# Where the first batch's stacked keys and queries come from: part-by-part copies within SBUF, or scratch memory

## What is computed

```
q = (h @ wq.T + bq_).reshape(bh, sl, H, DH)
k = (h @ wk.T + bk_).reshape(bh, sl, H, DH)
scores = jnp.einsum('blhd,bmhd->bhlm', q, k) * inv_sqrt_d
w_avg = jax.nn.softmax(scores, axis=-1).mean(axis=1)
new_w = jax.nn.softmax(CSCALE * w_avg + rel[None], axis=-1)
sa = jnp.einsum('blm,bme->ble', new_w, h)
```

## Time and profile before

| what | us |
|---|---|
| median of three executions | 2780.65 |
| lowest, highest | 2773.95, 2781.83 |
| span of the profiled execution, first to last instruction | 2799.2 |
| last scatter of expert rows issued by POOL | 504.86 |
| fence matmul | 506.05 |
| first score matmul | 514.52 |
| last score matmul starts | 2661.6 |

### The profile page before, as it was taken

The page is one execution under the profiler, slowest core; times in us unless marked ns, Lnnn a source line. Parts: engine busy times, 40 slices in busy tenths (PEclk is TensorE's granted clock), DMA queues, the critical chain, the costliest instruction groups (busy, mean ns, idle before and its releaser), DMA issues.

```text
span 2799.2 us, 93828 instructions
## 1 busy us (share of the span) xinstructions
PE 2390.9 (85%) x38289; PEld 1272.3 (45%) x38289; DVE 2454.6 (88%) x3428; ACT 2303.4 (82%) x4212; POOL 1447.9 (52%) x2877
## 2 busy tenths in 40 slices
PE   5778777689898999999899998999989988989856
PEld 3445365234444444444444454444444444444435
DVE  4887944699998999999999999999999998999956
ACT  5887634489898999999999999999999988989832
POOL 3445553235654566445664466644665446643564
PEclk8898887699999999999999999999999999999977
DMA  4000023322212121221212212122131221210000
GB/s 134 1 1 1 23 78 94 75 44 50 47 20 47 37 58 33 34 47 35 59 30 37 48 33 61 24 43 46 32 63 20 48 42 36 41 26 11 2 1 16
DMA packets 49198, 110.44 MB, mean 39 GB/s; under 512 B 7424, under 2 KB 42112, under 8 KB 44480
## 3 DMA queue, kind: packets, MB, share of 16 engines
q1 hardware_dynamic: 40384, 96.31, 17.2%
q0 software_dynamic: 2432, 5.08, 0.6%
q10 hardware_dynamic: 5952, 3.04, 0.4%
HBM read 79.41 MB, written 29.05 MB: 39 GB/s over the span
## 4 chain that ended last, share of the span: by engine, by line
PE 41%; issue 18%; ACT 12%; DVE 11%; POOL 8%; DMA 1%; ACTq 0%; SPq 0%; DVEq 0%; POOLq 0%
PE bank L773 13%; PE bank L704 12%; PE bank L784 11%; ACT E L1046 9%; DVE NM L1423 7%; ACT acc L997 1%; POOL acc L1644 1%; POOL H L1654 1%; PE bank L685 1%; POOL H L1657 1%; PE bank L698 1%; POOL smp L1637 1%; ACT UB L1008 1%; POOL dg L1702 1%; PE bank L747 0%
## 5 line engine op out<-in xcount | busy, mean ns | idle before, releaser
L1423 DVE TENSOR_REDUCE NM<-bank 128x1 f32<-128x1024 f32 x1536 | 1800.3, 1207 | 97.0 <-PE bank L773 76.5
L1046 ACT ACTIVATE E<-bank,NM 128x1024 f32<-128x1024 f32 x1536 | 1709.0, 1119 | 198.1 <-DVE NM L1423 153.1
L773 PE MATMUL bank<-KS,QS 72*32 72x512 bf16 x12288 | 977.7, 390 | 173.7 <-ACT E L1046 118.5
L784 PE MATMUL bank<-E,dg 128*32 128x256 f32 x12288 | 943.7, 387 | 8.0 <-issue 6.2
L1702 POOL TENSOR_TENSOR dg<-mask,RZ 128x128 f32<-128x128 f32 x384 | 153.7, 400 | 871.9 <-DVE RZ L1433 766.8
L773 PEld LDWEIGHTS bank<-KS,QS 72*32 72x32 bf16 x12288 | 263.2, 96 | 713.4 <-ACT E L1046 583.9
L784 PEld LDWEIGHTS bank<-E,dg 128*32 128x32 f32 x12288 | 394.6, 112 | 300.4 <-issue 75.3
L1046 ACT ACTIVATION_READ_ACCUMULATOR E<-bank,NM 128x1 f32 x1536 | 310.0, 202 | 0.0
L1644 POOL TENSOR_TENSOR acc<-acc,rel 128x256 f32<-128x256 f32 x384 | 272.8, 731 | 7.8 <-ACT acc L997 7.8
L704 PE MATMUL bank<-H,ET 128*32 128x129 f32 x6144 | 193.8, 276 | 9.7 <-DVE ET L1366 6.3
L704 PE MATMUL bank<-hT,WL 128*32 128x256 f32 x2304 | 166.5, 389 | 29.0 <-ACT UB L1008 21.9
(11 more groups left out here) (265 smaller groups left out, 2639.1 us busy)
## 6 DMA issues: line engine op xcount, KB each, us to landing
KS<-scratch SPq DMA_DIRECT2D x72, 384.0 KB
QS<-scratch SPq DMA_DIRECT2D x216, 128.0 KB
scratch<-UB SPq DMA_DIRECT2D x144, 128.0 KB
WL<-in_wl SPq DMA_DIRECT2D x6, 1091.0 KB, 12.4
first<-in_fill SPq DMA_DIRECT2D x2, 990.0 KB, 8.1
second<-in_fill SPq DMA_DIRECT2D x2, 990.0 KB, 10.3
UNITB<-second ACTq DMA_DIRECT2D x2, 528.0 KB
W<-in_moe_w SPq DMA_DIRECT2D x1, 1032.0 KB
```

Source lines behind the costliest of these rows:

```text
L773: inst = PE_.matmul(bank[x % 3][32 * i:32 * i + 32, k * 512:k * 512 + 512], QS[0:72, half % 2, 4 * hq + i, r0:r0 + 32], KS[0:72, b, k, 4 * ...
L784: inst = PE_.matmul(pb(6)[32 * k:32 * k + 32, 256 * grp:256 * grp + 256], dg[:, x // 4 % 3, x % 4, :], E[:, x % NE, :].rearrange("p (i k c ...
L1046: A_.activation(E[:, x % NE, :], bank[x % 3][:, :], ACT.Exp, bias=NM[:, x % 4:x % 4 + 1], accum_out=ZS[:, quad % 3, j:j + 1]).then_inc(s[" ...
L1423: V.tensor_reduce(NM[:, x % 4:x % 4 + 1], bank[x % 3][:, :], AX.X, ALU.max, negate=True).then_inc(s["rowmax"], 1)
```

## The change

For halves 0 and 1, SP no longer stores the parts and reads them back. New functions `place_k` and `place_q` issue nine DMAs each, from a plane of `PQ` (128 partitions of 1 KB) straight to 8 partitions of `KS` or `QS` (16 KB each). So that a plane's partitions lie in the order in which the stack takes them (all heads of dimension 0, then of dimension 1, ...), the columns of the weights and the biases are permuted on the host (`by_d`). The stores of later halves then write DRAM in the order in which it lies, without a swap. All waits are counted anew; `part0` of half 1, and the first of POOL's pieces for half 2, wait for the copies' own semaphores.

```diff
+        def stacked_k(b, l):
+            return 48 * (l + 1) + (96 if b == 0 else 0)
+        def stored(n):
+            return 96 * (n - 1)
...
                 if k:
                     e.wait_ge(s["parts"], 4 * n + 18)
                 elif n > -4:
-                    e.wait_ge(s["pq_store"], 96 * (4 + n))
+                    e.wait_ge(s["stackk00"], 144)
+                    e.wait_ge(s["stackq00"], 144)
...
                     e.wait_ge(s["pjo"], 2 * n + 10)
-                    e.wait_ge(s["pq_store"], 96 * (4 + n))
+                    if n == -2:
+                        e.wait_ge(s["stackk01"], 144)
+                        e.wait_ge(s["stackq01"], 144)
+                    else:
+                        e.wait_ge(s["pq_store"], stored(3 + n))
...
+            e.wait_ge(s["split"], before_half(n - 4) + 16)
             for j in range(3):
-                if n < 2:
-                    e.wait_ge(s["parts"], 4 * n + (1, 3, 4)[j])
-                else:
-                    e.wait_ge(s["split"], before_half(n - 4) + 16)
                 for k in range(2):
-                    e.dma_start(scr[b, hf, k, j].rearrange("d h t -> h d t"), PQ[:, 2 * j + k, :]).then_inc(s["pq_store"], 16)
+                    e.dma_start(scr[b, hf, k, j], PQ[:, 2 * j + k, :]).then_inc(s["pq_store"], 16)
+
+        def place_k(e, n):
+            for j in range(3):
+                e.wait_ge(s["parts"], 4 * n + (1, 3, 4)[j])
+                for i in range(3):
+                    r0 = 24 * i + 8 * j
+                    e.dma_start(KS[r0:r0 + 8, 0, n, :, :], PQ[:, 2 * j + 1, :]).then_inc(s[f"stackk0{n}"], 16)
+
+        def place_q(e, n):
+            for i in range(3):
+                e.wait_ge(s["parts"], 4 * n + (1, 3, 4)[i])
+                for j in range(3):
+                    r0 = 24 * i + 8 * j
+                    e.dma_start(QS[r0:r0 + 8, n, :, :], PQ[:, 2 * i, :]).then_inc(s[f"stackq0{n}"], 16)
...
             for n in range(2, HALF_N):
-                stack_q(e, n - 1)
+                if n > 2:
+                    stack_q(e, n - 1)
                 store_qk(e, n)
...
             mixed_of(0)
-            store_qk(e, 0)
-            stack_k(e, 0)
-            stack_q(e, 0)
-            store_qk(e, 1)
-            stack_k(e, 1)
+            place_k(e, 0)
+            place_q(e, 0)
+            place_k(e, 1)
+            place_q(e, 1)
             mixed_of(1)
             fence_sp(e, 1)
```

More of the change, by code:

```diff
@@ L764, in scores @@
                 if x % 128 == 0:
-                    e.wait_ge(s[f"stackk{b}0"], 48 * (l + 1))
-                    e.wait_ge(s[f"stackk{b}1"], 48 * (l + 1))
+                    e.wait_ge(s[f"stackk{b}0"], stacked_k(b, l))
+                    e.wait_ge(s[f"stackk{b}1"], stacked_k(b, l))
                 if x % 64 == 0:
@@ L1004, in post_act @@
                 if fc == 0:
-                    e.wait_ge(s["pq_store"], 96 * min(4 + n, HALF_N))
+                    e.wait_ge(s["pq_store"], stored(min(3 + n, HALF_N - 1)))
                     if n:
@@ L1755, in stack_k @@
             l, b, hf, u = unit(n)
-            e.wait_ge(s["pq_store"], 96 * (n + 1))
+            e.wait_ge(s["pq_store"], stored(n))
             if l:
@@ L1764, in stack_q @@
             l, b, hf, u = unit(n)
-            e.wait_ge(s["pq_store"], 96 * (n + 1))
-            if n >= 2:
-                e.wait_ge(s["scores"], 64 * (n - 1))
+            e.wait_ge(s["pq_store"], stored(n))
+            e.wait_ge(s["scores"], 64 * (n - 1))
             for i in range(3):
@@ L1776, in store_qk @@
                 e.wait_ge(s[f"stackq{b}{hf}"], 144 * l)
-                e.wait_ge(s[f"stackk{b}{hf}"], 48 * l)
+                e.wait_ge(s[f"stackk{b}{hf}"], stacked_k(b, l - 1))
+            e.wait_ge(s["split"], before_half(n - 4) + 16)
             for j in range(3):
-                if n < 2:
-                    e.wait_ge(s["parts"], 4 * n + (1, 3, 4)[j])
-                else:
-                    e.wait_ge(s["split"], before_half(n - 4) + 16)
                 for k in range(2):
-                    e.dma_start(scr[b, hf, k, j].rearrange("d h t -> h d t"), PQ[:, 2 * j + k, :]).then_inc(s["pq_store"], 16)
+                    e.dma_start(scr[b, hf, k, j], PQ[:, 2 * j + k, :]).then_inc(s["pq_store"], 16)
[11 more added lines that the diff above has]
+                    e.dma_start(QS[r0:r0 + 8, n, :, :], PQ[:, 2 * i, :]).then_inc(s[f"stackq0{n}"], 16)
         def rows_of(e, r):
@@ L1916 @@
     q = "L1_attn_"
+    by_d = np.arange(128).reshape(16, 8).T.reshape(128)
     wl = np.concatenate([
-        g[q + "Wq"].transpose(0, 2, 1), g[q + "Wk"].transpose(0, 2, 1), g[q + "W1"].transpose(0, 2, 1),
+        g[q + "Wq"].transpose(0, 2, 1)[:, :, by_d], g[q + "Wk"].transpose(0, 2, 1)[:, :, by_d], g[q + "W1"].transpose(0, 2, 1),
         g[q + "W2"].transpose(0, 2, 1).reshape(6, 4, 128, 128).transpose(0, 2, 1, 3).reshape(6, 128, 512),
@@ L1921 @@
           ("ln1_w", "ln1_b", "ln2_w", "ln2_b", "ln3_w", "ln3_b", "b2")],
-        g[q + "bq"][:, :, None], g[q + "bk"][:, :, None], g[q + "b1"].reshape(6, 4, 128).transpose(0, 2, 1),
+        g[q + "bq"][:, by_d, None], g[q + "bk"][:, by_d, None], g[q + "b1"].reshape(6, 4, 128).transpose(0, 2, 1),
     ], axis=2)
```

## The result

In nine runs each on one chip the changed kernel took **2791.30 us** (2781.94 to 2807.70), the kernel before 2781.83 us (2773.95 to 2790.61). The medians lie 9.5 us apart. The forecast was +13.4.

A forecast was written before the change was run, and what follows sets the result against it. The prediction took the bound to be the 8.28 us idle before the first score, waiting for half 1's keys. 17.9 + 2 - 8.1 + 1.6 = +13.4 us on the median 2780.65 gave 2794 us, range 2773 to 2807.

The forecast's parts named there:

- forecast case: Copies at the seam take 1.29 to 2.08 us each: +4.4 to +27 us, 2785 to 2808; chance 0.5.
- Term 1: At the seam, ACT's first piece of half 1 waits for half 0's 18 copies: 502.35 instead of 484.45, +17.9 us.
- d: Time of one 128 KB copy into 8 partitions when copies run back to back, taken as 1.7 us.
- the middle of a range between a quiet and a crowded row: Copy time taken between query reads in a crowded queue (1.29 us) and with nothing else about (2.08): 1.7 us.
- Term 2: After ACT's wait, PE restarts at the low clock, slowing two to three expert units: +2 us.
- Term 3: The idle before the first score matmul goes, since half 1's keys land ahead of the fence: -8.1 us.
- one of the signs that I had named as wrong: At the first score, a wait for `KS` still ahead of it would show the forecast wrong.
- Term 4: The load of Y stands behind half 1's 18 copies in SP's queue, so DVE waits for it: +1.6 us.
- The later halves at no cost: Unswapped stores in the 22 later halves change no time, since existing waits cover them: 0 us.
- Rival A: Copies at the seam are fast (up to 1.02 us each), ACT waits 0 to 5.7 us: 2772.5 to about 2779; chance 0.25.
- Rival B: Copies run at the query reads' quiet rate throughout, 2.08 us each, Y late by 8.4: +27 us, 2808; chance 0.2.

The follow-up runs named there:

- e2: The changed kernel with half 1's parts in a buffer of their own, so ACT waits for no copy: 2794.50 us, 0.9993 of the kernel before.
- e13: The changed kernel with each copy going into 8 partitions spaced 9 apart instead of 8 neighbours: 2766.67 us, 0.9946 of the kernel before.
- e6: The changed kernel with 36 more copies of 128 KB, in four destination shapes, while the DMA engines are idle: 2794.09 us in one run.
- e1: The changed kernel with Y loaded before half 1's nine query copies, not after: 2802.14 us, 1.0019 of the kernel before.
- e9: The kernel before with each half's nine query reads into 8 partitions written as three into 24: 2772.78 us, 0.9975 of the kernel before.
- e10: The kernel before with three wide query reads per half and unswapped stores with permuted weights: 2763.71 us, 0.9943 of the kernel before.

## Why the prediction was right, and where it was not

The forecast of 2794 us lay 2.7 us above the measured median, in the forecast case and with its mechanism. That it is so close is luck: the seam lost 7 us more than the sum said, and the halves after it gave back 10 us that the sum had at nothing.

- **Term 1, ACT's wait (forecast +17.9).** It measured 37.2 - 15.8 = +21.4. The mechanism is confirmed by e2 and e13. The fixed part of 2.0 us was right (1.9 in e6); what was mis-sized is d, (36.1 - 2.0) / 18 = 1.89 and not 1.7, which makes up the whole 3.5 us. The step that failed is the middle of a range between a quiet and a crowded row. The quiet rate of the query reads (2.08) and the quiet copies of e6 (2.04) lie close together, and the 1.29 from the crowded queue came from subtracting guessed shares for keys and stores. Nor does other traffic speak for a value below the quiet one: beside the unit rows the copies took 2.4 us each, and only after them 1.4.
- **Term 2, the low clock (+2).** From ACT's piece to the start of the fence's matmuls were 19.9 us after (488.14 to 508.05) and 21.6 before, so -1.7. The clock did fall to 0.50 for 5.7 us. In neither profile does PE wait for a unit row in this stretch; before, it stopped three times for 0.70 to 0.82 us with nothing that it waits for in the profile, and after it did not. That covers 2.3 us; the rest of the difference stays open.
- **Term 3, the idle at the first score (-8.1).** It fell by 5.1 only, 8.28 to 3.20, and a wait for `KS` was one of the signs that I had named as wrong. The keys of half 1 landed after the fence: from ACT's piece to just before 511.44 are 23 us, where I had 18.4 and the fence at 23.8. With 1.1 us to the first issue and 2.0 fixed, the nine copies took 2.2 us each, not 1.7; that the scatters beside them slowed them is not shown, since copies with nothing beside them took 2.0 in e1. And the fence came 3.7 us sooner than in my sum (20.1 us after the piece).
- **Term 4, Y (+1.6).** 8.72 us, of which 6.4 are on the path (e1). Y landed 42.9 us after ACT's piece and not 36.3. SP issued its load only at 516.24, after 4.6 us of waiting for the last scatter, a wait that the sum does not have. But by the times of the packets in the trace the copies of half 1 moved until about 529, 40 us after their first issue or 2.1 us each, and Y landed 2 us behind them. So here too it is d that was too small, and the transfer of Y itself was about as I had it.
- **The later halves at no cost.** This step failed. "Even a store twice as slow would be read by nobody earlier" is true of waits on the store, and SP's wait for POOL did cover it. But the stores without their swap made the 20 halves 9.3 us shorter in the profiles, and 9 us lie between e9 and e10 by the runs. The likely way is that a store or read also occupies DMA engines, and PE can be held by that without waiting for its data.
- **Sum.** Forecast 17.9 + 2 - 8.1 + 1.6 = 13.4. By the profile the first score is at +14.6 (21.4 - 1.7 - 5.1), mark 1 at +20.5 with Y, then -1.4 and -9.3: +9.8.

Rival A needed d up to 1.04; the spaced rows of e13 came near it (d = 1.12), and there the seam is 3 us ahead of the route through scratch. Rival B's d of 2.08 was a little too high for the copies of half 0 and right for those of half 1, and its late Y of 8.4 us was the measured one. The rule of the Trainium skill on the port swizzle ("SBUF — State Buffer", Door 1), which I weighed and bounded by the trace, pointed the right way (e6, e13), with 54 GB/s where e6 shows 66 and the end of half 0's copies 107.

## What to carry to other kernels

A copy within SBUF is not cheap because it stays on the chip: look at how many partitions it goes into and where they lie, and if the order of rows is free, as it is in a contraction, space them. When a buffer's reuse waits for a copy, the copy's landing is on the compute path; the six stores, landed 9 us after their first issue, were not. A second buffer takes it off again. And cost every DMA twice: for who waits for its data, and for how many DMA engines it fills, since PE may be held by that as well.

## What was unexpected of the hardware

- The issuing engine itself seems to be held while the copies before are not done: SP 2.2 us per copy (19.68 us for nine, the nine before them 6.28), ACT 20.69 us for nine, during which ACT computed nothing.
- A load of 66 KB took 5.4 us beside the copies into neighbours, 2.9 beside the spaced ones and 2.3 without copies.
- Eight partitions 9 apart instead of neighbours took the copy from 1.89 to 1.12 us at the seam; 16 apart, in the quiet stretch, from 2.04 to 1.24.
- The same copy into 8 neighbours took 2.4 us beside the unit rows, 1.4 right after them, 2.0 in a quiet stretch of its own and 1.2 in e2; why is open.
- Three reads into 24 partitions each used a third of the DMA share of nine reads into 8 (0.16 beside 0.47, over 19.2 us), at the same bytes and in about the same time.
- PE stopped for 2.9 us with no wait that the profile shows while query reads ended, and then ran 4.9 us at the lower clock.
